# FFN steps of a two-layer transformer kernel on Trainium2: low parts ahead of a tile's statistics, weight signs in two halves, one weight block behind each rotation on GpSimd

## The reference, cut to what matters

```python
x = x + _L0_attn_ref(xn, ...) + _L0_ffn_ref(xn, ...)
xn = _layernorm(x, axis=-1)
x = x + _L1_attn_ref(xn, L1_attn_w_qkv, L1_attn_w_o) + _L1_ffn_ref(xn, L1_ffn_w_fc, L1_ffn_w_proj)
# in _L1_ffn_ref: bitlinear = layer_norm, then a product with sign(round(w / mean|w|)) * mean|w|
h = bitlinear(x, w_fc)                    # 256 -> 1024
h = jax.nn.gelu(h, approximate=False)
return bitlinear(h, w_proj)               # 1024 -> 256
```

## Time and profile before

| what | value |
|---|---|
| median of 3 runs | 386.6 us (385.39 to 388.68) |
| the profiled execution, its time | 387.23 us |
| the profiled execution, its span | 385.4 us |
| TensorE busy in the span | 369.0 us (96%) |
| VectorE, ScalarE, GpSimd busy | 307.1, 250.0, 279.4 us |
| mean granted TensorE clock | 0.996 of full speed |

### The profile page before, as it was taken

The page is one execution under the profiler, slowest core; times in us unless marked ns, Lnnn a source line. Parts: engine busy times, 40 slices in busy tenths (PEclk is TensorE's granted clock), DMA queues, the critical chain, the costliest instruction groups (busy, mean ns, idle before and its releaser), DMA issues.

```text
span 385.4 us, 8456 instructions
## 1 busy us (share of the span) xinstructions
PE 369.0 (96%) x2888; PEld 343.6 (89%) x2888; DVE 307.1 (80%) x684; ACT 250.0 (65%) x804; POOL 279.4 (72%) x238
## 2 busy tenths in 40 slices
PE   8998889989999998999999999999999999999995
PEld 3667779979899997999999999999999999998985
DVE  6878999876999885779777888787788879788882
ACT  1368855573987764667667676757666667767671
POOL 3437759789999996977779897667997777776000
PEclk9999999999999999899999999999999999999999
DMA  7996112513444345443345643334565343333300
GB/s 261 414 408 284 27 30 55 138 43 81 110 99 96 79 108 130 112 109 80 87 110 120 157 110 92 93 92 98 131 149 142 93 104 83 84 83 86 79 2 27
DMA packets 34219, 45.15 MB, mean 117 GB/s; under 512 B 5505, under 2 KB 25986, under 8 KB 33794
## 3 DMA queue, kind: packets, MB, share of 16 engines
q1 hardware_dynamic: 34032, 44.62, 43.1%
q10 hardware_dynamic: 146, 0.00, 0.0%
HBM read 13.14 MB, written 1.05 MB: 37 GB/s over the span
## 4 chain that ended last, share of the span: by engine, by line
PE 67%; POOL 15%; DVE 9%; SPq 3%; DMA 2%; ACT 2%; issue 2%; POOLq 0%
PE bank L1287 14%; PE bank L1250 11%; PE bank L1307 10%; PE bank L1004 10%; PE bank L1200 10%; PE bank L1253 3%; POOL woT_lo L606 3%; POOL rope_a L669 2%; POOL split_lo L670 2%; POOL split_hi L668 2%; POOL rope_b L660 2%; PE bank L1013 2%; DMA wq0T<-in_L_attn_w_qkv_dram 2%; PE bank L1159 2%; POOL rope_a L658 2%
## 5 line engine op out<-in xcount | busy, mean ns | idle before, releaser
L515 ACT ACTIVATE bank<-bank,neg_max 128x256 f32<-128x256 f32 (+1 forms) x256 | 101.3, 397 | 10.0 <-DVE neg_max L911 9.9
L524 ACT ACTIVATE probT_hi<-bank 128x512 fp32r<-128x512 f32 x96 | 57.6, 600 | 73.6 <-PE bank L1004 73.4
L911 DVE TENSOR_REDUCE neg_max<-bank 128x2 f32<-128x512 f32 (+1 forms) x96 | 65.9, 687 | 31.2 <-PE bank L1253 30.9
L1287 PE MATMUL bank<-probT_hi,v 128*128 128x256 f32 x384 | 76.4, 295 | 0.6 <-DVE oT_lo L939 0.6
L660 POOL TENSOR_TENSOR rope_b<-turned,cst 128x512 f32<-128x512 f32 x36 | 47.1, 1308 | 40.6 <-DMA turned<-raw 40.6
L1250 PE MATMUL bank<-kT,qT 128*128 128x256 f32 (+1 forms) x512 | 73.4, 276 | 1.7 <-DMA qT<-split_lo 1.7
L927 DVE TENSOR_TENSOR prob<-bank,rsum 128x512 f32<-128x512 f32 x96 | 66.4, 691 | 3.3
L1250 PEld LDWEIGHTS bank<-kT,qT 128*128 128x128 f32 x512 | 66.5, 191 | 1.9 <-DMA qT<-split_lo 1.9
L933 DVE TENSOR_TENSOR probT_lo<-bank,probT_hi 128x512 fp32r<-128x512 f32 x96 | 65.4, 681 | 0.5 <-ACT probT_hi L524 0.4
L1287 PEld LDWEIGHTS bank<-probT_hi,v 128*128 128x128 f32 x384 | 58.6, 189 | 3.5 <-issue 2.2
L1004 PE MATMUL bank<-cst,prob 128*128 128x128 f32 x384 | 58.4, 275 | 2.2 <-DVE prob L927 2.2
(11 more groups left out here) (158 smaller groups left out, 735.2 us busy)
## 6 DMA issues: line engine op xcount, KB each, us to landing
turned<-raw SPq DMA_DIRECT2D x144, 64.0 KB, 2.0
qT<-split_hi SPq DMA_DIRECT2D x64, 128.0 KB, 2.4
qT<-split_lo SPq DMA_DIRECT2D x64, 128.0 KB, 2.4
wq0T<-in_L_attn_w_qkv_dram SPq DMA_DIRECT2D x4, 512.0 KB, 7.9
wout<-in_L_attn_w_out_dram SPq DMA_DIRECT2D x4, 512.0 KB, 12.4
nat_qkv<-in_L_attn_w_qkv_dram SPq DMA_DIRECT2D x2, 1024.0 KB, 20.5
nat_o<-in_L_attn_w_o_dram SPq DMA_DIRECT2D x1, 2048.0 KB, 21.4
kT<-split_hi SPq DMA_DIRECT2D x16, 128.0 KB, 2.4
```

What stands on the lines that cost most here:

```text
L515: ins = nc.scalar.activation(own, own, ACT.Exp, bias=neg_max[it % 2][:, first + j:first + j + 1], accum_out=sums[it % 2][:, first + j:firs ...
L524: nc.scalar.activation(probT[0][:, n % 4, :], bank[2 + n % 2][:, :], ACT.Copy).then_inc(t_hi, 1)
L911: dve.tensor_reduce(neg_max[n // UNITS % 2][:, unit_columns(n % UNITS)], score_bank(n)[:, :].rearrange("p (h k) -> p h k", h=heads), AX.X, ...
L1287: ins = pe.matmul(group_bank(), v[b % 2][:, DH * z:DH * z + P], p, start=m == 0, stop=m == last)
```

## The change

Four things change.

- VectorE: in step s the statistics are those of tile s - 1 instead of tile s, and stand behind that tile's two low parts; `hidden_stats(0)` and `hidden_scale(1)` move from ahead of step 1 into it, and `hidden_scale` stands ahead of the statistics instead of at the end of a step (steps 1, 2 and 3, for batches 1, 2 and 3).
- ScalarE: the signs of the projection weights are made in two halves of 1024 columns in step 1, one ahead of `gelu(1)` and one behind `empty`, instead of whole in step 0. `proj(0)` and `column_sums` wait for both. `HI_IN` puts weight block 3 into step 0, and brings blocks 6, 8 and 11 a step forward.
- GpSimd: the first rotations and roots change places, so that a rotation's products run ahead of a root, and from block 4 on one weight block stands behind each rotation instead of two behind each of the blocks 4 to 7.
- No instruction is added or taken away but one: the second half of the signs.

```diff
-        HI_IN = {1: 4, 2: 5, 3: 6, 4: 8, 5: 9, 6: 11, 7: 12}
+        HI_IN = {0: 4, 2: 5, 3: 7, 4: 9, 5: 10, 6: 12, 7: 12}
...
                 hidden_hi(step - 1, 1)
+                if step == 1:
+                    sign(2, nat_proj[:, 0:4, :], projT[:, 0:4, :], tern_proj)
                 if step < TILES:
                     gelu(step)
...
-                if step == 0:
-                    sign(2, nat_proj[:, :, :], projT[:, :, :], tern_proj)
+                if step == 1:
+                    sign(2, nat_proj[:, 4:8, :], projT[:, 4:8, :], tern_proj)
...
+            weights_lo(3, 4)
+            rope_products(0)
             tile_root(0)
-            weights_lo(3, 4)
+            rope_sums(0)
             tile_root(1)
-            rope_products(0)
+            weights_lo(4, 5)
+            rope_products(1)
             tile_root(2)
-            weights_lo(4, 5)
-            rope_sums(0)
+            rope_sums(1)
+            weights_lo(5, 6)
             tile_root(3)
-            rope_products(1)
-            weights_lo(5, 6)
-            tile_root(4)
-            rope_sums(1)
-            tile_root(5)
             weights_lo(6, 7)
             rope_products(2)
-            tile_root(6)
+            tile_root(4)
             rope_sums(2)
             weights_lo(7, 8)
+            tile_root(5)
+            weights_lo(8, 10)
+            rope_products(3)
+            tile_root(6)
+            rope_sums(3)
             tile_root(7)
-            rope_products(3)
-            rope_sums(3)
-            weights_lo(8, 10)
+            weights_lo(10, 11)
             for n in range(4, len(BLOCKS)):
                 rope_products(n)
                 rope_sums(n)
-                weights_lo(2 * n + 2, min(2 * n + 4, len(W_UNITS)))
+                weights_lo(n + 7, min(n + 8, len(W_UNITS)))
...
-            hidden_stats(0)
-            hidden_scale(1)
             for step in range(1, STEPS):
                 t = step - 1
                 if t < TILES:
                     hidden_lo(t, 0)
                     hidden_lo(t, 1)
                 if step in (1, 2):
                     tokens_lo(step + 1)
-                if step < TILES:
-                    hidden_stats(step)
+                if step <= 3:
+                    hidden_scale(step)
+                if t < TILES:
+                    hidden_stats(t)
                 if t >= 1:
                     hidden_factors(t - 1)
                     ffn_add(t - 1)
-                if step in (1, 2):
-                    hidden_scale(step + 1)
...
-                    pe.wait_ge(tern_proj, 1)
+                    pe.wait_ge(tern_proj, 2)
```

## The result

The changed kernel takes 387.75 us (median of 20 runs, 385.15 to 389.58) beside 386.56 us for the kernel before (20 runs, 385.05 to 388.68). The ratio is 1.0039, with a 95% interval of 1.0023 to 1.0055: slower, by 0.4%. The forecast was 384.9 us. The result lies inside the range and the 1%, on the wrong side of zero.

The account below looks back on a forecast made before the run. TensorE was taken as the bound, busy 369.0 of 385.4 us. Slots -3.38, VectorE 0.0, clock +1.67 and steps 7 and 8 at 0 made -1.7, so 384.9 us from the median 386.6; range 381.6 to 388.2.

Parts of the forecast that it names:

- the 1%: Whole kernel: time stays within 3.9 us of the kernel before, given a chance of 0.74.
- VectorE's term in step 1: FFN step 1: proj(1) starts at 58.3 as before, with both hidden_scale at 3.4 us; 0.0, from -2.1 to +2.0.
- The slots' term: Attention slot 21: block 9 lands in time, so the wait of 1.71 and the slow clock's 1.67 go; -3.38 us.
- The lower end that I gave (-1.71): Slot 21: only the wait is saved, if the slow clock comes anyway; -1.71 us.
- The path forecast: GpSimd ends block 8 up to 3.75 us earlier, at 135.2; SyncE's chain follows and block 9 lands at 148.6.
- ScalarE, 0: Step 1: the split signs cost nothing and tokens_hi(2) ends 0.45 earlier, at 47.25; at most 1.0 if cover went.
- by position: Step 2: hidden_scale(2), near 54, sits out GpSimd's work for about 1.2 us, judged from where it falls.
- The clock ahead of proj(1): TensorE waits 2.2 us at proj(1) and a slow stretch of the clock follows; +1.67, ends 0 and 1.67.
- Steps 7 and 8: Addition ahead of proj(6) 0.7 earlier, L874 0.5 dearer, proj(7) tight; together 0, from -0.7 to +1.8.
- C: Rival: sitting out GpSimd's instructions delays proj(1), proj(6) and proj(7), with two slow stretches; +3.8, 390.4 us, chance 0.18.
- the positions come out in the middle: Argument against the slower rival: VectorE's small instructions fall between the best and worst places beside GpSimd's instructions.

Follow-up runs that it names:

- e1: Kernel before with one weight block behind each rotation from block 4 on instead of two, FFN steps untouched: 384.02 us, ratio 0.9937.
- e2: Changed kernel with two weight blocks behind the rotations of blocks 4 to 7 again: 388.14 us, ratio 1.0047.
- the second execution: Profiled execution of the changed kernel, unedited, timed once more beside others: 387.83 us, span 386.0; median of that run 387.86 us.
- e3: Changed kernel with hidden_scale and the tile's second scale taking one factor as a scalar operand instead of a second SBUF tensor: 384.1 us, ratio 0.9953.
- e6: Changed kernel with 14 products that nobody reads on TensorE ahead of its wait at proj(1): 385.91 us, ratio 1.0002.
- e10: Changed kernel with VectorE's old order and the scalar-operand forms of e3: 383.79 us, ratio 0.9926.
- e7: Kernel before with only VectorE's new order, ScalarE and GpSimd as before: 390.1 us, ratio 1.0099.
- e8: Changed kernel with VectorE's old order, ScalarE, GpSimd and the slots as changed: 388.8 us, ratio 1.0087.
- e5: Kernel before with both the single weight block behind each rotation and the scalar-operand forms: 384.61 us, ratio 0.9955.
- e9: e3 with both halves of ScalarE's signs behind the tile's transfers in step 1: 382.96 us, ratio 0.9928.

## Why the prediction was wrong, step by step

Two terms of the sum failed. VectorE's term in step 1 stood at 0.0 and measured +1.25, since `hidden_scale` sits out more of GpSimd's work than its position was taken to say. The slots' term stood at -3.38, and on the medians the one-block edit is worth -1.4 to -2.4 alone, since the slow stretch behind the hole was counted in full. Neither alone turns the sign of -1.7; the two together do.

- **The slots, -3.38.** The hole is gone, and the account shows -3.54, but neither the size nor the path was right. The 1.67 of slow clock were taken from one execution and carried over to the median, where e1 shows 1.4 to 2.4 us for the whole term. The lower end that I gave (-1.71) was the one to take. The path forecast was a block 8 that is 3.75 us earlier, at 135.2. e1 has that in the kernel before; in the changed kernel it issues 4.4 us later than that, where I had left 2.1 of slack. Between 44 and 145 us GpSimd waits there 6.7 us for `turned` and 1.4 for `raw`, and waited for neither in the kernel before. And e2 shows that it was no term that adds to the others: once the steps are late, the hole is covered anyway.
- **ScalarE, 0.** Half true. The signs themselves hid, but tokens_hi came later than worked out: VectorE idled 1.05 to 1.13 us instead of 0.8 (low parts of the tokens at 47.46 in the second execution, forecast 47.25). That is 0.21 of the 1.25 at proj(1).
- **VectorE, 0.0 (-2.1 to +2.0).** Mis-sized by 1.25. The mechanism was right: the price of `hidden_scale` was rightly named as what decides, and e3 shows it, as 3.5 us go with the second inputs. hidden_scale(1) was forecast at 2.2 and took 2.04 to 2.14; hidden_scale(2) was put at 1.2 "by position" and took 2.30 to 2.31 in both executions. Together they took 4.44 instead of 3.4, which with the 0.21 makes the 1.25. A position worked out to half a microsecond, against instructions of 1.3 us that follow each other without a gap, decides nothing. Beside such a run of GpSimd the two dependent two-input instructions took about 2 us all four times, one remainder and one whole.
- **The clock ahead of proj(1), +1.67.** Right: 3.32 us of wait (forecast 2.2), 1.49 of loss, and e6 gives it back.
- **Steps 7 and 8, 0 (-0.7 to +1.8).** The additions came 0.20 and 0.46 later instead of about in time. The L877 of tile 6 took 1.08 to 1.17 us, 0.9 to 1.0 more than its 0.16 elsewhere where 0.5 more was forecast, the one of tile 7 0.60 to 0.61. Inside the bounds.
- **Not in the sum:** 0.65 us more wait at slot 10 for `prob`, which is 0.99 in the changed kernel and 0.34 in the one before. e1 (0.60) and e10 (0.88) have it too. Its reason wasn't tried.

By its sum, then: -3.54 + 1.25 + 1.49 + 0.66 + 0.74 = +0.6 between the two profiled executions, where -1.7 was forecast: it lacked 1.25, 0.66 and 0.74 of loss, and the slots and the clock came out 0.34 better than it had them. Against an execution of before in which the hole cost only its 1.7 it would be 2.3; the medians show 1.2. Of the rivals it was C, which had 0.18, near the halfway point that I gave for it (387.9; the middle of its ends 384.9 and 390.4 is 387.65). Its condition was stated right, that the steps lose more than the slots give. Its price was lower than feared, because only one of the two slow stretches came. The argument against it, that "the positions come out in the middle", was no argument.

What the parts do together is shown by the runs. VectorE's order gives the steps 1.9 to 2.6 us and makes GpSimd late (e7, +1.0%). GpSimd's order of the steps cures little of that: block 8's first DMA issues at 142.14 in e7 and at 142.41 in e2, which has both orders (some 1.4 less without its slow stretch at the start), where it was 138.94. With VectorE's old order it takes away GpSimd's waits ahead of the roots, in which VectorE's two-input instructions went undisturbed (e8, +0.9%). Both orders with the slots stand at +0.4%. Without the second inputs the whole change is worth -0.5% (e3), and -0.7% with VectorE's old order (e10). The one-block edit alone gives the kernel before as much (e1, -0.6%), so the ratios show no gain from the other parts of the change. At a mean clock of 0.998 or more e1, e5 and e10 took 383.58 to 384.07 us and e3 and e9 382.3 to 383.13. That hints at some 1 us from VectorE's new order once the second inputs are gone, from seven executions in all; GpSimd's order in the steps shows nothing there either.

## What to carry to other kernels

Before an engine order is tightened so that GpSimd no longer pauses beside VectorE's small instructions, look through these for those with two tensor inputs in SBUF; where one factor is a column of one value a partition, give it as a scalar operand, which cost 0.21 to 0.27 us here instead of up to 1.3. When a gain includes a slow stretch of the clock, price it by several executions and not by the profiled one: the mean clock beside each time sorts them. And do not add the gain of a hole late in the span to a loss early in it: the loss covers the hole.

## What the runs showed of the hardware that was not expected

- `tensor_scalar` with a second factor read from SBUF as a scalar takes 210 to 271 ns on average over steps in which GpSimd is busy most of the time (e3), where `tensor_tensor` on the same data takes 348 to 720 ns on average and `scalar_tensor_tensor` 1243 (the changed kernel).
- The length of a wait on TensorE does not tell by itself whether the lower clock follows. In the profiled executions waits of 1.71 (before, slot 21), 1.83 (e5), 1.99 (e3), 2.22 and 2.38 (e7) and 2.65 us (e8) were followed by it, and waits of 1.79 (e10), 1.87 (the changed kernel), 2.29 (e9) and 2.33 us (e8) were not. Those of 3.3 us were followed by it in all three profiled executions that had them (the changed kernel twice, with 1.49 us of loss each, and e2). With fourteen products that nobody reads in place of the wait the clock stayed at 1.0 (e6).
